# Two chained graph networks on one core: residuals handed over in the rows-of-x buffers, and a shared-out end

## The reference

```python
x = _layernorm(x + L0(x, adj))     # first network, gated
x = _layernorm(x + L1(x, adj))     # second network, softmax
# one layer of L0: bilinear scores of the rows (m_left above the diagonal, m_right below), then
attention = exp(u) * adj / (row sum + 1e-10)
h = relu(layer_norm(attention @ (h @ W_lin.T + b)) * ln_a + ln_b)
# one layer of L1:
attn = softmax(h @ h.T / sqrt(D)) * adj / (row sum + 1e-10)
ctx = (attn above diagonal) @ hl + diagonal * hs + (attn below diagonal) @ hr
h = relu((ctx - mean) / sqrt(var + 1e-12) * g + beta)
```

## Time and profile before

| | us |
|---|---|
| median of 3 runs | 1717.54 (1716.96 to 1718.06) |
| the profiled execution | 1716.51 |
| its span, first to last instruction | 1714.9 |

### The profile page before, as it was taken

The page is one execution under the profiler, slowest core; times in us unless marked ns, Lnnn a source line. Parts: engine busy times, 40 slices in busy tenths (PEclk is TensorE's granted clock), DMA queues, the critical chain, the costliest instruction groups (busy, mean ns, idle before and its releaser), DMA issues.

```text
span 1714.9 us, 29860 instructions
## 1 busy us (share of the span) xinstructions
PE 1667.0 (97%) x9664; PEld 1579.3 (92%) x9664; DVE 1267.7 (74%) x2785; ACT 948.4 (55%) x1985; POOL 614.6 (36%) x658
## 2 busy tenths in 40 slices
PE   7999999999999999999989999999999999999994
PEld 6989989899898889889889999999999999999994
DVE  4587685867859578695876877769687696877866
ACT  4545455464554645546556665655655656656653
POOL 5143252432424233243522523525143351523503
PEclk9999999999999999999999999999999999999997
DMA  7015012020300203003013040300304003030101
GB/s 230 1 32 157 6 48 75 24 92 6 104 19 24 92 6 116 6 24 93 21 61 96 22 95 0 102 15 22 95 3 114 1 22 96 22 95 0 64 14 37
DMA packets 108015, 92.19 MB, mean 54 GB/s; under 512 B 63280, under 2 KB 101168, under 8 KB 107952
## 3 DMA queue, kind: packets, MB, share of 16 engines
q1 hardware_dynamic: 107952, 91.51, 18.6%
HBM read 66.33 MB, written 25.17 MB: 53 GB/s over the span
## 4 chain that ended last, share of the span: by engine, by line
PE 51%; issue 32%; POOL 10%; DVE 3%; ACT 2%; SPq 1%; DMA 1%; POOLq 0%; ACTq 0%; DVEq 0%
PE b_work L1157 34%; PE b_work L1170 8%; POOL g_qv_lo L621 3%; POOL b_ht L601 3%; PE b_score_ps L119 3%; PE b_work L372 2%; PE b_score_ps L386 1%; PE b_work L396 1%; POOL g_keep_l L616 1%; POOL g_sigma L630 1%; POOL g_a_nat L617 1%; POOL g_frstd L634 1%; PE b_turn L1114 1%; PE b_score_ps L1133 1%; PE b_score_ps L1130 0%
## 5 line engine op out<-in xcount | busy, mean ns | idle before, releaser
L1157 PE MATMUL b_work<-b_w_hi,b_ht 128*128 128x384 f32 x2304 | 607.0, 338 | 8.3 <-ACT b_work L1256 8.3
L1157 PEld LDWEIGHTS b_work<-b_w_hi,b_ht 128*128 128x128 f32 x2304 | 418.6, 188 | 10.0 <-ACT b_work L1256 9.4
L1157 PE MATMUL b_work<-b_w_lo,b_ht 128*128 128x384 f32 x1152 | 385.9, 335 | 0.0
L372 PE MATMUL b_work<-b_ht,b_w_hi 128*128 128x512 f32 x1152 | 357.7, 392 | 9.5 <-DVE b_w_lo L696 9.5
L372 PEld LDWEIGHTS b_work<-b_ht,b_w_hi 128*128 128x128 f32 x1152 | 216.3, 189 | 51.2 <-issue 9.5
L621 POOL TENSOR_TENSOR g_qv_lo<-g_v_full,g_qv_hi 128x384 fp32r<-128x384 f32 x128 | 133.4, 1062 | 361.0 <-ACT g_qv_hi L495 361.0
L372 PE MATMUL b_work<-b_ht,b_w_lo 128*128 128x512 f32 x576 | 225.8, 392 | 0.0
L1494 DVE TENSOR_TENSOR s_v_lo<-b_work,s_v_hi 128x384 fp32r<-128x384 f32 x256 | 139.3, 554 | 116.1 <-ACT s_v_hi L1262 114.5
L1157 PEld LDWEIGHTS b_work<-b_w_lo,b_ht 128*128 128x128 f32 x1152 | 217.1, 188 | 0.0
L728 DVE TENSOR_TENSOR g_qv_lo<-b_work,g_qv_hi 128x512 fp32r<-128x512 f32 x192 | 128.8, 687 | 111.1 <-ACT g_qv_hi L483 109.2
L396 PE MATMUL b_work<-b_w_hi,b_ht 128*128 128x384 f32 x768 | 206.2, 336 | 0.0
(11 more groups left out here) (142 smaller groups left out, 3247.6 us busy)
## 6 DMA issues: line engine op xcount, KB each, us to landing
b_x_in<-in_x_t SPq DMA_DIRECT2D x16, 768.0 KB, 7.2
g_x_res<-in_x SPq DMA_DIRECT2D x16, 768.0 KB, 7.5
x<-b_z SPq DMA_DIRECT2D x16, 768.0 KB, 3.9
b_x_in<-x SPq DMA_DIRECT2D x64, 192.0 KB, 6.7
s_x_res<-x SPq DMA_DIRECT2D x16, 768.0 KB, 6.9
out<-b_z SPq DMA_DIRECT2D x15, 768.0 KB, 4.1
b_a_tr<-in_adj_t SPq DMA_DIRECT2D x64, 64.0 KB, 3.4
g_a_nat<-in_adj SPq DMA_DIRECT2D x32, 64.0 KB, 2.4
```

Source lines behind the costliest of these rows:

```text
L372: mm = pe.matmul(bank[:], w, h, start=(n == 0), stop=(n == len(pairs) - 1))
L1157: mm = pe.matmul(bank[:, 0:H], h, w, start=(n == 0 and side == 2), stop=(n == len(pairs) - 1), skip_group_check=True)
```

## The change

**Hand-over.** The residual of the first network's last pass is written into `x_res[s]`, the buffer that holds the rows of x (now kept for both streams beyond the first network), and normalised and stored from there; `z[0]` and `z[1]` are free at once, so `contexts_out` of the second network's units 0 and 1 no longer waits for a store. The tail is spread over units 0 to 3 of the second network's first pass: in unit 0 stream 0's residuals and two of stream 1's gain-and-shift tiles, in unit 1 the other two and stream 1's residuals, in unit 2 all statistics, and on ACT `gated_normalise(0)` at the end of unit 2 and `gated_normalise(1)` at the end of unit 3. `weight_hi(0)` and `weight_hi(1)` stand behind unit 0; all three `weight_lo` on POOL stand in unit 0 of the pass, behind the root and the diagonal; SP issues the first weight loads at once and the x1 stores inside its first pass. DVE's first pass is written out in full.

**End.** Stream 0's tail leaves DVE: relu on ACT (`other_relu`), residual on POOL (`other_residual`), sums and sums of squares on ACT (`other_sums`, with results in the free x input buffers), root and offset on POOL (`other_statistics`), the scaled copy on ACT (`other_normalise`). Stream 1's variances are taken in halves of two tiles, between the context rows, and POOL takes the root by halves. The last store is cut in three, tile 0, tiles 2 and 3, tile 1.

```diff
-        x_res1 = late("x_res1", [P, NT, H])
+        x_res = [late(f"x_res{s}", [P, NT, H]) for s in range(STREAMS)]
...
@@ first network, DVE, up_to_contexts, last unit
                 if not more:
-                    add_residual(i, s)
+                    for t in range(NT):
+                        context_stats(i, unit, t, more)
+                    return
...
@@ first network, DVE, class Tail
+                def residual(s, t):
+                    dve.wait_ge(res_loaded[s], 16 * PASSES)
+                    dve.wait_ge(scaled, (PASSES - 1) * (STREAMS * NT) + s * NT + t + 1)
+                    nc.vector.scalar_tensor_tensor(x_res[s][:, t, :], z[s][:, t, 0:H], 0.0, x_res[s][:, t, :],
+                                                   ALU.max, ALU.add).then_inc(summed, 1)
...
@@ SP
             sp.wait_ge(folded, 1)
-            store_last(0)
             load_weight(0)
             load_weight(1)
             sp.wait_ge(split, 1)
             load_weight(2)
-            store_last(1)
             sp.wait_ge(split, SIDES)
...
+                    if first:
+                        store_last(s)
...
@@ ACT, unit 0 of the second network
             seed(0, 0, 6)
-            gated_normalise(0)
             value_hi(0, 0, 3)
             value_hi(0, 0, 4)
             seed(0, 0, 7)
-            weight_hi(0)
             value_hi(0, 0, 6)
...
             copy_part(0, 1)
+            weight_hi(0)
             weight_hi(1)
...
@@ ACT, second_half
-                if tail:
-                    gated_normalise(1)
...
                 if more:
                     copy_part(i, unit + 1)
+                if tail == 1:
+                    weight_hi(2)
+                if tail in (2, 3):
+                    gated_normalise(tail - 2)
...
@@ ACT, last unit
+                        other_relu(i)
+                        other_sums(i, (0, 1))
                         normalise(i, unit, range(LAST_GT))
+                        other_sums(i, (2, 3))
+                        other_normalise(i)
+                        final_normalise(i)
...
@@ POOL, last unit
+            def last_steps(i):
+                s = STREAMS - 1
+                other_residual(i, (0, 1, 2))
+                half_roots(i, 0)
+                other_residual(i, (3,))
+                times_gain(i, s, 0)
+                half_roots(i, 1)
+                plus_shift(i, s, 0)
+                other_statistics()
+                final_roots(i, s, count=0)
...
@@ DVE, up_to_contexts of units 1 (tail 1) and 2 (tail 2) of the first pass
+                    if tail == 1 and j < 5:
+                        gated.gain_and_shift(j - 1)
+                    if tail == 2:
+                        gated.final_stats(0, j - 3)
...
+                if tail == 1:
+                    gated.residual(1, 0)
...
+                if not more:
+                    contexts_out(i, unit, (0, 1))
+                    half_variances(i, 0)
+                    contexts_out(i, unit, (2,))
+                    last_deviations(i)
+                    contexts_out(i, unit, (3,))
+                    half_variances(i, 1)
+                    return
```

More of the change, by code:

```diff
@@ L1098, in _ @@
             for s in range(STREAMS):
[L1099 removed]
+                sp.wait_ge(stored[s], before[s] + 16 * (PASSES + 2 * s))
         @block.tensor
@@ L1420, in one_pass @@
                     layer, s = divmod(unit, STREAMS)
-                    more = not (last and unit == UNITS - 1)
+                    if last and unit == UNITS - 1:
+                        last_steps(i)
+                        break
                     roots(i, unit)
-                    if first and unit == 0:
+                    if first and unit == 2:
                         gated_final_roots(1)
@@ L1429, in one_pass @@
                     if layer == 1:
-                        for t in range(NT if more else LAST_GT):
-                            gain_and_shift(i, s, t)
+                        for t in range(NT):
+                            times_gain(i, s, t)
+                            plus_shift(i, s, t)
                             if t == 1:
                                 diagonal(i, unit + 1)
-                    elif more:
+                    else:
                         diagonal(i, unit + 1)
                     if first and unit == 0:
+                        weight_lo(0)
+                        weight_lo(1)
                         weight_lo(2)
-                    if layer == 1:
+                    if layer == 1 and not last:
                         final_roots(i, s)
+                    if first and unit == 1:
+                        gated_final_roots(0)
                     if not last and unit % STREAMS == 1:
@@ L1520, in own_probability, with contexts_out @@
                 nc.vector.tensor_reduce(own[:], expo[:], AX.X, ALU.add).then_inc(own_ready, 1)
-            def contexts_out(i, unit):
+            def contexts_out(i, unit, tiles=range(NT), first=False):
                 layer, s = divmod(unit % UNITS, STREAMS)
-                if layer == 0:
+                if layer == 0 and not first:
                     dve.wait_ge(stored[s], before[s] + 16 * (i + unit // UNITS))
                 dve.wait_ge(own_ready, nth(i, unit, 1, 0))
-                for t in range(NT):
+                for t in tiles:
                     j = VB + t
@@ L1636, in up_to_contexts @@
                     final_var(i, s)
-                contexts_out(i, unit)
+                contexts_out(i, unit, first=tail == 1)
                 if s is not None:
@@ L1669, in lower_layer, with upper_layer, end @@
                 begin(i, 1)
-            def end(i, s):
-                unit = UNITS - 1
-                variances(i, unit)
-                deviations(i, unit)
-                last_gain_and_shift(s)
-                add_residual(i, s, range(NT), LAST_GT)
-                final_stats(i, s)
-                final_var(i, s)
-                final_offset(i, s)
-                final_normalise(i, s)
+            def upper_layer(i, last=False, first=False):
+                go_on(i, 1, last, first)
+                begin(i, 2)
+                go_on(i, 2, last, first)
+                if not last:
+                    begin(i, 3)
+                    go_on(i, 3, first=first)
+            def end(i):
+                unit, s = UNITS - 1, STREAMS - 1
+                last_gain_and_shift(s, range(LAST_GT, NT // 2))
+                dve.wait_ge(rstd_ready, nth(i, unit, 1, 0) + 1)
+                last_gain_and_shift(s, range(NT // 2, NT))
+                last_residual(i)
+                final_var(i, 0)
+                final_offset(i, s, count=0)
+                final_normalise(i, s, count=0)
             gated.variances()
```

245 lines of the change are left out of this document (163 added, 82 removed).

## The result

The changed kernel took 1704.2 us (median of 4 runs, 1703.78 to 1705.33) against 1717.62 for the kernel before on the same chip: ratio 0.9925, 95% interval 0.9909 to 0.9941, 13.4 us less. The forecast was 1702.3 in a range of 1699 to 1708; rival B had stood at 1705.0. The profiled execution took 1703.78 us with a span of 1702.2, 12.7 less than the one before.

What follows compares the result with a forecast made beforehand. PE, busy 97% of the span, could gain only where it stands still: the hand-over (9.5 us) and the DVE-bound end (5.7). Together 15.2 us off 1716.51 gave 1701.3, or 1702.3 for the median; range 1699 to 1708.

Steps and rivals of the forecast that it cites:

- rival B: At the end, POOL is the bound through slow small steps, stores meet; end gives 3 us, 1705.0; 12 in 100.
- Hand-over, first stop: Unit 0's first PE stop: residuals and statistics leave DVE's list before the context statistics; 3.0 us gained, 1.5 to 3.5.
- Clock: PE's half-speed stretch after the first stop goes; 1.2 us gained, from 0 to 1.6.
- Second and third stop, wait before the scores: Unit 0: normalised copy moved, 1.7 us; no weight waited for, 3.3 us; longer wait before the scores, 0.6 lost.
- term 5: End of unit 0: DVE becomes the later one, wait of 0.38 before the scores grows to about 1.0; loses 0.6.
- Case A: DVE is the bound of units 0 and 1; the hand-over then gives 5.5 us, 1706.3; 20 in 100.
- Cover of what is moved: Units 1 to 3: moved weights, copies, statistics and stores fit in without PE waiting; no loss in the sum.
- The end: After PE's last products: earlier context rows, gain and shift, and split store give 5.7 us, from 3 to 6.3.
- the halved variances: At the end, cutting the variances in halves adds one more set of small steps, about 0.4 us.
- The last store: Store in three parts: first leaves earlier, last carries a quarter; 0.3 us gained, from -0.4 to 0.8.
- The shared SBUF interface: DVE's two-input steps in unit 1 are slow beside POOL; term kept at nothing, up to 2 us in the range.
- Case D: Shared interface slows every moved step in units 0, 1 and the end; 1730.5, slower from 1.14 us mean; 3 in 100.

Runs made afterwards that it cites:

- e_end: The kernel before with only the changed end: 1714.42 us, ratio 0.9983 against the kernel before.
- e_unroll: The kernel before with VectorE's loop over the passes begun one pass later, its first round written out in front: 1718.48 us in one run.
- e_weight_first: The kernel before with the load of the second network's first weight in front of the store of stream 0's x1: 1715.0 us, ratio 0.9984.
- e_stats: The changed kernel with stream 1's last two statistics and final variance steps moved on VectorE behind the maximum for unit 3: 1702.65 us.
- e_shift: The changed kernel with the statistics moved behind the maximum for unit 3, plus eight unread 128x1 memsets there on VectorE: 1701.08 us in one run.

## Why the prediction was right, and where it was not

The places of the gain were right: PE's three stops and the end. The size was right by luck in part. Against the sum of 15.2 us the spans gave 12.7: 11.8 at the hand-over up to the scores for unit 2 for 9.5 forecast, then 2.5 lost where nothing was forecast, 0.4 in the first network, and 3.0 for 5.7 at the end. The measured 1704.2 is 1.9 us above the forecast and only 0.8 below rival B's 1705.0, which had 12 chances in 100; the range held because it was drawn to take in A and B.

**Hand-over, first stop** (3.0 forecast): 3.22. By the traces DVE's residuals in front of the context statistics were the cause (no run takes them out alone), and ACT's copy is the next bound: PE still waits 0.34 for the seed.

**Clock** (1.2, from 0 to 1.6): the fall is gone, as said. Unit 0 took 27.05 us with 5.75 of stops in it, so 21.3 of work, and 19.38 without stops: 1.9, which is 0.7 over the term; whether slow matmuls or the restarts behind three stops made it, the traces don't tell. The forecast took the third stop to be without a fall, from one trace; in `e_end` it has one that costs 1.8 us, and in `e_unroll` one with 20 matmuls in the same 6 us. If some executions of before have it too, which their spread suggests and no trace of before shows, that is why the change gave 13.4 in medians and 12.7 in profiles.

**Second and third stop, wait before the scores** (1.7 + 3.3 - 0.6): all 5.75 us went, 1.35 more than forecast. The step that failed here is term 5 (a loss of 0.6 before the scores): DVE does not become late, since two gain-and-shift pairs and three statistics left its list there for one residual more. The third stop hung on the first weight for 2.2 of its 3.3 us, and on DVE for the rest as that list then stood (`e_weight_first`). **Unit 1** (0.9): 0.87. Case A's condition, DVE as the bound of units 0 and 1, did not arise.

**Cover of what is moved** ("cost nothing"): wrong by 2.46 us, and its own sign of being wrong came, a new wait of PE in units 1 to 3 (1.60 us in unit 3). "Unit 2 gains eight statistics ... about what a unit with its own tail carries" compared sums of work and not the place: the last four and the small steps of stream 1 stand in front of the context rows, and behind these stands the maximum for unit 3, on which ACT's exponentials and seeds hang. That cost 1.85, with the held step of 1.12 us (`e_stats`). The other 0.6 was in no term: the place of the instructions in DVE's program (`e_shift`). ACT's copies, the weights and SP's order show no wait of PE's, as said.

**The end** (5.7): 3.0. The context rows come 3.68 earlier, counted from PE's last matmul (3.95 forecast). Then the mis-sized term, the halved variances at 0.4: the rows and small steps took 7.07 us up to the first gain step, where 5.6 were laid out. The first set of small steps takes 0.55, the offset step 0.47 and the second set 1.34. Two small steps took 0.55 and 0.68 beside POOL (0.17 for the second's like in the first set), and 0.24 was idle. So the offset is 3.79 earlier and not 5.4. The last store, +0.3 forecast, is -0.78: rival B's small steps are 0.45 to 0.53 us, neither my 0.15 nor its 0.95, and with the long power they delay the 768 KB until it meets the last stores. B's figure for the end, 3, is the measured one. Its chain came about in part: the stores meet, but ACT's four copies for stream 0 end at 1695.78, just before DVE's last offset (1695.82) lets ACT begin with stream 1. Of the 2.7 missing us the late offset makes 1.6 and the stores 1.1. The surplus of the hand-over's first units covered the loss behind them, not this one.

**The shared SBUF interface.** The rows show it in both directions: DVE's 128x4 step at 1.12 for 0.16 until the masks end, POOL's power at 3.16 for 1.01 beside DVE's residuals. The Trainium skill (SBUF — State Buffer, Who interferes with whom) calls it an exclusive lock: whichever instruction comes first has it to its end and the other is blocked, so order decides and not shape. On DVE's side the traces agree, to 0.01 us at the masks. On POOL's side they show more than one instruction's wait: the 3.16 reach over one step of L1672 and four of L1684. The forecast had priced only large steps and none on POOL's side. Of the four large steps in unit 1 that it named, two took 1.08 and 1.26 us beside POOL's low halves, and PE did not wait for them, as the forecast had it. Case D's price did not arise: it needed a mean of 1.14 us a step, and most of the moved steps took 0.5 to 0.6.

## What to carry to other kernels

When work is moved off a stall, ask which instruction of the next stage now stands behind it, not whether the engine's sum still fits: the same statistics cost 1.85 us in front of the rows that the next maximum stands behind, and no wait of PE's 7 us later on the same engine.

A last large store belongs well ahead of the last small ones: count from the transfer rate when it must be issued. A small elementwise step is not small on GpSimd (0.45 to 0.53 us here), nor always on VectorE while GpSimd runs (0.55 to 1.29 us at places here, instead of some 0.16).

Differences under 1 us between two versions of a long program can come from where its instructions lie; an edit that moves them and does nothing else is the control.

## What was not expected of the hardware

- Eight unused memsets of 128x1 in an idle of VectorE took away its idle 150 us and more later: 0.46 us at the first boundary, 0.22 at every later one, and 0.24 at the end. In the changed kernel the profile shows one transfer of an instruction queue between 1080 and 1084 us and none in before's at that boundary; later rounds with 0.22 have none. The Trainium skill (Runtime: NRT & Kernel Launch, Instruction fetch mechanics) says that each engine fetches its program in blocks ahead of time and that a jump outside what is held makes it wait. No run here shows that this is the cause.
- The same stop of 3.2 to 3.3 us was followed by a clock of 1.00 in one execution and by 0.57 and 0.53 over 6 us in two others (of `e_end` and `e_unroll`).
- The same first network, in two executions, reached the hand-over's scores at 841.70 and 843.51 us; 1.4 of the 1.8 arose at its first loads.
- A GpSimd power of 128x4 took 1.01, 1.23, 1.33 or 3.16 us, to the hundredth the same in all four traces where it was 3.16 (three kernels).
- VectorE steps of 128x4 with a single SBUF input were held beside GpSimd's masks too: L780, 0.17 us at the median, took 0.94 in the changed kernel at 848.33.
